# GpSimd's last ten weight remainders: one 512-column instruction each, or four of 128 columns

## The reference, cut to what matters

```python
x = x + tanh(g_xattn) * xattn(layernorm(x), ctx, ctx, Wq, Wk, Wv)     # retention
xf = layernorm(x)
scores = softmax(xf @ Wg.T); expert_weights, expert_indices = top_k(scores, 2)
h1 = xf @ W1[e].T + (xf @ A1[e].T) @ B1[e].T + b1[e]
h3 = xf @ W3[e].T + (xf @ A3[e].T) @ B3[e].T + b3[e]
g  = silu(h1) * h3
y_e = g @ W2[e].T + (g @ A2[e].T) @ B2[e].T + b2[e]
x = x + tanh(g_ffn) * sum_e gates[t, e] * y_e
```

## Time and profile before

| what | value |
|---|---|
| median of 3 executions | 343.44 us |
| profiled execution | 341.12 us |
| its span, first to last instruction | 339.3 us |
| outside the span | 1.8 us |
| low parts on GpSimd (L907) | 48, of which 10 behind the batch loop (122.0 to 151.1 us of the span) |
| granted TensorE clock, mean | 0.978 of full speed |

### The profile page before, as it was taken

One profiled execution on the slowest core, in us unless ns is written; L12 is line 12 of the kernel. 1 busy time (PEld: TensorE's weight loads), 2 busy tenths in 40 slices (PEclk: granted clock), 3 DMA queues, 4 the chain that ended last, 5 costly groups with the idle time before them and its releaser, 6 DMA issues.

```text
span 339.3 us, 7418 instructions
## 1 busy us (share of the span) xinstructions
PE 301.0 (89%) x1738; PEld 230.9 (68%) x1758; DVE 260.4 (77%) x685; ACT 190.7 (56%) x406; POOL 207.9 (61%) x245
## 2 busy tenths in 40 slices
PE   8669889799998778987999989999999999999970
PEld 4558768578786634765667757777777777777750
DVE  2679875979889879887798887877787778777850
ACT  4636754666787527656574545564556555655540
POOL 1558876778894084886465646665675666566341
PEclk9979999999999699999999999999999999999997
DMA  7926897999785075646576757776652233244100
GB/s 276 388 72 204 238 289 197 289 292 254 266 258 178 6 233 186 186 111 203 127 195 151 207 148 189 199 195 160 185 132 46 48 61 49 49 57 61 19 0 0
DMA packets 30424, 54.35 MB, mean 160 GB/s; under 512 B 7233, under 2 KB 15809, under 8 KB 30113
## 3 DMA queue, kind: packets, MB, share of 16 engines
q1 hardware_dynamic: 16128, 38.99, 35.2%
q0 software_dynamic: 7488, 9.36, 17.1%
q10 hardware_dynamic: 6768, 5.54, 5.3%
HBM read 41.92 MB, written 10.65 MB: 155 GB/s over the span
## 4 chain that ended last, share of the span: by engine, by line
PE 39%; DVE 19%; DMA 10%; POOL 9%; issue 9%; ACT 6%; SPq 3%; DVEq 2%; POOLq 1%; ACTq 0%
PE bank L610 21%; PE bank L627 11%; POOL WL L907 5%; DMA xs<-x_in 5%; PE bank L618 3%; DMA out<-ys,cols 3%; DVE stage L1016 3%; DMA WH<-lora_in 2%; PE bank L600 2%; ACT WH L719 2%; SPq L353 2%; DVE g L1418 1%; DVE h L1418 1%; DVE st L1031 1%; DVE x L1095 1%
## 5 line engine op out<-in xcount | busy, mean ns | idle before, releaser
L986 POOL DMA_INDIRECT out<-ys,cols x39 | 63.5, 1628 | 64.8 <-DVE gsel L1402 18.8
L907 POOL TENSOR_TENSOR WL<-stage,WH 128x512 bf16<-128x512 f32 x48 | 61.4, 1327 | 20.8 <-ACT WH L719 20.7
L610 PE MATMUL bank<-WH,xh 128*128 x156 | 55.7, 438 | 0.8 <-ACT xh L833 0.6
L971 POOL DMA_INDIRECT xg<-xn_rows,colg x39 | 40.0, 1025 | 21.1 <-DVE colg L1246 10.8
L610 PE MATMUL bank<-WH,xl 128*128 x156 | 49.0, 395 | 0.0
L719 ACT ACTIVATE WH<-stage 128x512 fp32r<-128x512 f32 x48 | 29.5, 630 | 26.5 <-DVE stage L1016 25.3
L610 PE MATMUL bank<-WL,xb 128*128 x137 | 42.9, 384 | 1.3
L870 ACT ACTIVATE ys<-BA,gsel 128x256 f32 x23 | 11.7, 509 | 41.4 <-DMA out<-ys,cols 41.4
L627 PE MATMUL bank<-WH,gh 128*128 x156 | 31.9, 327 | 3.0 <-ACT gh L839 3.0
L610 PEld LDWEIGHTS bank<-WH,xl 128*128 128x128 f32 x156 | 29.2, 188 | 7.2 <-DVE xl L1408 0.4
L1424 DVE TENSOR_TENSOR g<-g,h 128x512 f32<-128x512 f32 x39 | 29.2, 748 | 5.3 <-ACT h L857 1.4
(11 more groups left out here) (218 smaller groups left out, 656.9 us busy)
## 6 DMA issues: line engine op xcount, KB each, us to landing
stage<-w_all_in SPq DMA_DIRECT2D x48, 256.0 KB, 4.6
BB<-biases_in SPq DMA_DIRECT2D x16, 640.0 KB, 4.4
BA<-biases_in SPq DMA_DIRECT2D x8, 640.0 KB, 4.1
LS<-WH SPq DMA_DIRECT2D x45, 48.0 KB
xs<-x_in SPq DMA_DIRECT2D x8, 256.0 KB, 4.1
cx<-ctxT_in SPq DMA_DIRECT2D x8, 256.0 KB, 4.2
out<-x ACTq DMA_DIRECT2D x8, 256.0 KB, 4.1
xn_rows<-xn ACTq DMA_DIRECT2D x8, 256.0 KB, 5.0
```

Source lines behind the costliest of these rows:

```text
L610: last = nc.tensor.matmul(dst[:, :], lhs[p][:, c * P:(c + 1) * P], W[:, bass.ds(e * (UNITS * UC) + (2 * kind + c) * UC, HID)], start=(part ...
L907: nc.gpsimd.tensor_tensor(w_dst(WL, s, m), stage[(u * UNITS + m) % NSTAGE][:], w_dst(WH, s, m).bitcast(F32), ALU.subtract).then_inc(s_wl, 1)
L971: nc.gpsimd.indirect_dma_start(out=xg[q][:], out_offset=None, in_=xn2_d[0:JA * P, :] if i < NA else xn2_d, in_offset=bass.IndirectOffsetOn ...
L986: nc.gpsimd.indirect_dma_start(out=out_rows, out_offset=bass.IndirectOffsetOnAxis(ap=cols[:, i:i + 1], axis=0), in_=ys[p][:], in_offset=No ...
```

## The change

The ten low parts behind the last batch step are each made by four instructions on 128 of the 512 columns. The wait stands before the first of the four and the signal on the last. The low parts in the batch loop stay whole.

```diff
+            def weight_lo_parts(s, u, m):
+                pool.wait_ge(s_wh, s * UNITS + m + 1)
+                lo, hi, raw = w_dst(WL, s, m), w_dst(WH, s, m), stage[(u * UNITS + m) % NSTAGE]
+                for a in range(0, UC, P):
+                    part = nc.gpsimd.tensor_tensor(lo[:, a:a + P], raw[:, a:a + P], hi[:, a:a + P].bitcast(F32), ALU.subtract)
+                part.then_inc(s_wl, 1)
+
...
             gather(0)
             gather(1)
-            weight_lo(E - 2, 0, 2)
-            weight_lo(E - 2, 0, 3)
+            weight_lo_parts(E - 2, 0, 2)
+            weight_lo_parts(E - 2, 0, 3)
             gather(2)
-            weight_lo(E - 2, 0, 4)
-            weight_lo(E - 2, 0, 5)
+            weight_lo_parts(E - 2, 0, 4)
+            weight_lo_parts(E - 2, 0, 5)
             for i in range(NT_SLOTS):
                 if i + XBUF - 1 < NT_SLOTS:
                     gather(i + XBUF - 1)
                 if i >= 1:
                     scatter(i - 1)
                 if i < 3:
-                    weight_lo(E - 1, 1, 2 * i)
-                    weight_lo(E - 1, 1, 2 * i + 1)
+                    weight_lo_parts(E - 1, 1, 2 * i)
+                    weight_lo_parts(E - 1, 1, 2 * i + 1)
```

## The result

The changed kernel is slower by 0.71%: the ratio to before is 1.0071, with a 95% interval from 1.0048 to 1.0095. Over 21 executions each the medians are 343.94 us and 342.07 us; 0.71% of 342 us is 2.4 us, the interval 1.6 to 3.2 us. The forecast was +2.9 us, +0.8%. A second series (the last experiment) gave 1.0069 (1.0029 to 1.0109). The ratio goes by the fast executions alone, so it is not that of the medians, which lie 1.9 us apart, and the two traced executions of the changed kernel (348.69 and 349.75 us) are slow ones.

A forecast was written before the change was run, and what follows sets the result against it. GpSimd's chain up to tile 2's scatter was taken to bound the changed stretch, TensorE from 200 us on. 2.7 + 0.2 + 0 = +2.9 us gave 344.0 us profiled, 346.3 us as median; range 342.0 to 349.5.

The forecast's parts named there:

- What bounds the stretch: From 134.4 to 154 us GpSimd is busy 16.18 of 19.60 us; its lateness at tile 2's scatter delays ScalarE and all after.
- The price of a piece: A 128-column low part takes 458 ns, 0.42 us in a row; a pair 0.9 us more; piece bounds 0.31 and 0.72 us.
- The pairs of expert 6: GpSimd's pairs at 122.04 and 125.94 end 0.9 and 1.8 us later, covered by TensorE's wait for ScalarE and later idling.
- The three pairs of expert 7: Pairs at 134.43, 140.91 and 147.99 in GpSimd's own chain: each one's 0.9 us counts in full, 2.7 us together.
- The collision with pair one: VectorE's L1424 of 137.20 now costs expert 7's first pair 0.6 us instead of the gather 0.41 us: +0.2 us.
- L1400 at 126.92: VectorE's gate column at expert 6's second pair still waits for two instructions, as does L1402: 1.66 against 1.57 us, taken as 0.
- the first rival: L1400 is kept out for all eight pieces, 1.7 us later: +4.6 us, 348.0 us; chance 0.28.
- The median: Profiled execution 344.0 us, plus the 2.3 us it had lain under the runs' median of 343.44: 346.3 us, +0.8%.
- The VectorE step that waits for all low parts: The step at 152.39 waits till about 154, covered by the 2.94 us that tile 4's silu has to spare before L870.
- The rule on the port: VectorE and GpSimd share an SBUF port; the skill says the first holds it one whole instruction, the 126.92 row showed two.

The follow-up runs named there:

- the last experiment: The changed kernel itself timed once more beside before, with nothing further changed: ratio 1.0069 (1.0029 to 1.0109).

## Why the prediction was right, and where not

**What bounds the stretch: right in the main.** GpSimd's chain of pairs, gathers and scatters sets scatter 2: in the changed kernel the view names no engine that GpSimd waits for ahead of the scatters 1 and 2 ("issue"). The runs with only expert 7 in pieces (slower) and with one pair taken off GpSimd (faster) agree with it from both sides. The chain that ended last runs through scatter 2 in before, in the run with expert 7 alone and in the second trace of the changed kernel; in the first trace it runs through the L1431 of 152.32 (4.21 us), which the same pair held up.

**The price of a piece: right.** 458 ns were worked out for 128 columns from three other widths, the median measured is 462; a pair of 3.4 us was forecast, 3.34 measured. The bounds (0.31 and 0.72 us) were not needed. The run with 64 columns fits the same line.

**The pairs of expert 6: the cover held.** TensorE's tile 0 still waited for ScalarE; with 64 columns the cover was gone, and TensorE waited for the low parts.

**The three pairs of expert 7: right.** 2.7 us forecast, 2.5 in the trace of the run that changes only them, 1.7 (0.7 to 2.7) in its time.

**The collision with pair one: smaller.** +0.2 us forecast: the pair paid 0.48 us (3.82 less 3.34) and the gather got 0.41 back (1.39 to 0.98), so +0.07 us.

**L1400 at 126.92: the step that failed.** I took 0, because it had waited for "two instructions" and would again. It waited for seven pieces, in each of the four traces with expert 6 in pieces of 128 columns, so the mechanism was the first rival's ("kept out"), short of it by the last piece: L1407 and L1409 took 2.83 + 0.28 = 3.11 us, where the forecast said 1.7 and that rival 3.3 or more. A count read from a run of two instructions could not tell "two" from "nearly to the end of the run". In the trace that costs 1.3 us, in the time of the kernel with expert 6 alone 0.4 us, uncertain by 0.8. The traces of the changed kernel add up to 3.8 us at scatter 2, 0.9 over the sum of 2.9, and the time to 2.4. So that the sum came out near the time is in part luck: the term put at 0 has 1.3 us in the trace, and the time shows less of it for a reason that the forecast did not have. The first rival's +4.6 us lies outside the interval all the same.

**The median.** 346.3 us was forecast and 343.94 measured. Of these 2.4 us, 1.4 are the start: three executions of before had a median of 343.44 us, 21 have 342.07.

**The VectorE step that waits for all low parts: the cover held.** In the first trace it found the low parts done (157.24, no idling), since VectorE itself had stood 4.20 us at L1431; in the second it waited 2.01 us, and ScalarE's L870 of that tile still idled 3.76 us for the scatter.

**The rule on the port.** The gate column got in at the next boundary when the second low part waited for the first (0.46 us) and in the run with 256 columns (0.77 us), but only behind seven pieces of 128 columns (2.83 us). The Trainium skill, "SBUF — State Buffer", section "SBUF: two separate sides", has the loser wait for the other's whole instruction. The first two agree with it; the third does not, nor do the L1407 and the L1431 that pieces of 256 columns kept out for one piece more (1.17 and 1.81 us), nor the L1400 of before (1.58 us, both low parts). The measurement decides: a boundary between instructions did not always free the port here.

## What to carry to other kernels

Cutting an instruction into pieces can pay only if the waiting engine gets in between them and the cutting engine has time to spare; look at the second first. In this kernel a fixed 0.15 us an instruction, on the engine that set the end, was a loss of 0.9 us a pair that could be worked out beforehand from three other widths. What helped was taking work off that engine and giving it to the one that had been waiting for it.

## What the runs showed that I had not expected

The gate column of tile 1 was kept out for seven of eight queued pieces of 128 columns in four executions out of four (2.80 to 2.83 us). Elsewhere in the same traces VectorE got in at the next boundary, with 128 columns (0.43 us, second trace) as with 256 (0.77 us), and with 256 it was also kept out for one piece more. With 64 columns L1409 stood 4.14 us, while an L1431 that asked at 147.62, 0.21 us after the record of a pair had begun, took 0.76 us, hardly longer than alone; that pair follows a scatter, behind which the first piece's record is some 0.6 us longer than another's, so the piece may not have computed yet. So the width of a piece does not decide it, and what does is not settled.

TensorE's filler ahead of tile 0 ran at either clock level. The busy time by stage, 121 to 125 us (length, busy of five engines, granted clock, DMA), in the run with only expert 7 in pieces:

```profile
121.00:125.00 4.00, 2.98 (x7) 1.17 (x8) 3.16 (x14) 1.11 (x4) 3.66 (x5) 0.50 0.51 147
```

The granted clock is 0.50 there, which is 1.2 GHz, and 1.00, 2.4 GHz, in the same stretch of before; the filler took 3.96 us instead of 2.54. Ahead of it, from 119 to 121 us, TensorE was busy 1.88 of 2.00 us at a granted 0.50 in that run and 1.55 us at 0.86 in before. Tile 0 starts some 1.5 us later in such executions, and where a kernel falls on the one side or the other no run here shows.
